# A two-layer graph network: first edge pass over a flat list of tiles, both ends gathered, its network layers a group apart, head sums four tiles at a time

## What is computed

```python
ms, mv = src_s[edge_src] + dst_s[edge_dst], src_v[edge_src] + dst_v[edge_dst]
h = silu(_ln(edge_scalars @ rw1 + rb1, rg1, rbe1))
h = silu(_ln(h @ rw2 + rb2, rg2, rbe2))
w = h @ rw3 + roff                       # 224 weights for each edge
Y1 = SQ3 * edge_vec * rsqrt(sum(edge_vec ** 2))
# products of w with ms, mv, the dot product and the cross product of mv and Y1
ls, lv = _eq_lin(ds, dv, lin_ws, lin_bs, lin_wv)
a = einsum('ehk,hk->eh', _smooth_leaky(alpha), alpha_dot)   # alpha: first 64 columns of ls
a = exp(a - segment_max(a)[edge_dst])    # over all edges with the same destination
ns = segment_sum(vs * a[..., None], edge_dst)     # and nv alike; divided by segment_sum(a)
```

## Time and profile before

| what | us |
|---|---|
| median of 3 runs (range) | 17817.21 (17774.64 to 17817.54) |
| the profiled execution's own time | 17828.81 |
| its span | 17826.9 |
| PE busy | 12392.4 (70%) |
| DVE busy | 10429.4 (59%) |
| ACT busy | 6609.0 (37%) |
| POOL busy | 4214.9 (24%) |
| mean granted TensorE clock | 0.779 of full speed |

### The profile page before, as it was taken

How to read it: one execution, slowest core, us unless ns; L and a number is a source line. 1 busy time by engine, 2 the same in 40 slices (tenths; PEclk the granted TensorE clock), 3 DMA queues, 4 the chain that set the end, 5 groups by cost and what they waited for, 6 DMA issues and landing times. The chain is left out here.

```text
span 17826.9 us, 270188 instructions
## 1 busy us (share of the span) xinstructions
PE 12392.4 (70%) x57506; PEld 9227.4 (52%) x57507; DVE 10429.4 (59%) x31035; ACT 6609.0 (37%) x17353; POOL 4214.9 (24%) x4337
## 2 busy tenths in 40 slices
PE   2488878888878888888862555444457777777776
PEld 1355555555555555555542444433336666666666
DVE  3366666666666666666666555533346666666663
ACT  0244444444444444444430000000025555555552
POOL 0021222122122222122211222200014444444440
PEclk7688888888888888888875666655559988888888
DMA  1121121111122112121222333300014444444443
GB/s 25 33 43 42 41 43 42 41 42 42 41 42 43 42 41 43 41 43 42 43 55 68 76 76 76 68 14 15 16 48 129 129 129 125 128 127 130 125 127 104
DMA packets 1816374, 1150.59 MB, mean 65 GB/s; under 512 B 1159827, under 2 KB 1540793, under 8 KB 1815742
## 3 DMA queue, kind: packets, MB, share of 16 engines
q1 hardware_dynamic: 1641278, 818.30, 17.2%
q0 software_dynamic: 174720, 329.09, 7.8%
HBM read 678.77 MB, written 467.83 MB: 64 GB/s over the span
## 5 line engine op out<-in xcount | busy, mean ns | idle before, releaser
L616 POOL DMA_INDIRECT att_src<-src_table,att_idx x1768 | 1769.4, 1001 | 6823.2 <-DMA att_idx<-in_src_dst 5501.5
L1660 POOL DMA_INDIRECT conv_src<-conv_table,conv_pair x1872 | 1840.6, 983 | 2309.8 <-DVE conv_prod L1820 1759.9
L1748 ACT ACTIVATE conv_scaled<-conv_onehot,conv_pair 128x128 f32<-128x128 f32 x5592 | 1659.1, 387 | 1251.2 <-DVE conv_onehot L1786 761.8
L666 PE MATMUL att_banks<-dst_feat,att_onehotT 128*128 x3528 | 973.0, 372 | 1313.1 <-issue 703.6
L1284 PE MATMUL attend_banks<-attend_wm,attend_onehot 128*128 128x168 f32 x3520 | 1009.3, 476 | 1099.5 <-DVE attend_onehot L1306 1099.5
L1284 PEld LDWEIGHTS attend_banks<-attend_wm,attend_onehot 128*128 128x128 f32 x3520 | 929.7, 320 | 1178.8 <-issue 1063.5
L666 PEld LDWEIGHTS att_banks<-dst_feat,att_onehotT 128*128 128x128 f32 x3528 | 584.0, 210 | 1752.7 <-issue 1752.7
L683 PE MATMUL att_banks<-att_w_last,att_hid 64*128 64x224 f32 x3528 | 1450.0, 499 | 13.0
L1690 PE MATMUL conv_banks<-conv_w_last,conv_hid 64*128 64x224 f32 x1858 | 656.8, 436 | 904.7 <-DVE conv_prod L1820 684.0
L697 PE MATMUL att_banks<-att_ident,att_ch 128*128 128x128 f32 (+1 forms) x5280 | 1240.8, 415 | 2.3 <-ACT att_chT L811 1.4
L1830 DVE SCALAR_TENSOR_TENSOR conv_acc<-conv_acc,conv_keep,conv_banks 128x320 f32<-128x320 f32 x1856 | 898.9, 509 | 541.8 <-PE conv_banks L1712 260.3
(11 more groups left out here) (353 smaller groups left out, 28846.2 us busy)
## 6 DMA issues: line engine op xcount, KB each, us to landing
agg<-conv_acc SPq DMA_DIRECT2D x928, 288.0 KB
messages<-att_msg SPq DMA_DIRECT2D x440, 320.0 KB
attend_msg<-messages SPq DMA_DIRECT2D x220, 640.0 KB, 4.0
conv_pair<-in_conv_rec SPq DMA_DIRECT2D x944, 70.0 KB
att_es<-in_esT SPq DMA_DIRECT2D x1776, 32.0 KB
conv_src<-conv_table,conv_pair POOLq DMA_INDIRECT x1872
att_idx<-in_src_dst SPq DMA_DIRECT2D x1768, 1.0 KB, 1.7
att_geo<-in_edge_vec SPq DMA_DIRECT2D x1768, 1.5 KB
```

Of the source, the lines that this page charges most:

```text
L616: g.indirect_dma_start(out=src[h][:, u, :], out_offset=None, in_=x_table[:, :], in_offset=bass.IndirectOffsetOnAxis(ap=idx[h][:, u, 0:1], ...
L666: last = t.matmul(banks[:, BM, n * FEAT:n * FEAT + FEAT], onehotT[:, u * P:u * P + P], dst_feat[:, bass.ds(b, 1), :].rearrange("p a f -> p ...
L1660: g.indirect_dma_start(out=src[q][:, u, 0, :], out_offset=None, in_=x_table[:, :], in_offset=bass.IndirectOffsetOnAxis(ap=ends[q][:, u // ...
L1748: last = s.activation(scaled[h][:, u, d, :], onehot[h][:, u, :], ACT.Copy, scale=geo[q][:, u // 2, u % 2, PLANE_AT[d]:PLANE_AT[d] + 1])
```

## The change

The first edge pass becomes its own function, `phase_attention`. It walks over a flat list of 1664 tiles (208 iterations of 8), each once, with no step table. The host packs node numbers and edge vectors of 8 tiles in one record and the edge scalars in one block, so that SP starts two loads an iteration, four iterations ahead. `phase_nodes_in` stores the destination rows as a second table in memory, and POOL gathers source and destination rows, 16 indirect DMAs an iteration, into four slots. The one-hots, their transposes and the matmul with `dst_feat` are gone from this loop. `nets` runs layer 1 for one group of 8 tiles and layer 2 for the group before it, so that one `roots` and one `normalise` serve both layers, 1024 columns wide. The hidden features go through the Silu function of another activation table: ACT loads one table ahead of `roots` and the other behind it, in every iteration. `edge_weights` takes rows 0 to 63 and rows 64 to 127 in turn, into two banks. The summing loop works with quads of 4 tiles that share a block: 520 steps of a quad (`QUAD_ITERS` = 130 iterations of 4 quads), PE adds the 4 products of a quad in PSUM, and DVE adds once for each quad. A quad whose edges end in several blocks is taken once for each, as tiles were. The core of the diff:

```diff
-ITERS = -(-(TILES + BLOCKS - 1) // ITER)
-STEPS = ITERS * ITER
-STEP_COLS = -(-(STEPS + 2 * ITER) // P)
-TABLE = STEP_COLS * P
+TURN = 4
+ATT_ITERS = TURN * (-(-TILES // (TURN * ITER)))
+ATT_TILES = ATT_ITERS * ITER
+QUAD = UNIT
+QUADS = ATT_TILES // QUAD
+QUAD_GROUP = 4
+QUAD_ITERS = 2 * (-(-(QUADS + BLOCKS - 1) // (2 * QUAD_GROUP)))
+QUAD_COLS = -(-QUAD_ITERS * QUAD_GROUP // P)
+QUAD_TABLE = QUAD_COLS * P
 NB = 7
 NODE_ITERS = BLOCKS // NB
...
+                    hold(sp, sp_passed, (dst_kept, i + 1))
+                    sp.dma_start(dr[i], out2[:, :, :]).then_inc(stored, 16)
...
-                        v.tensor_tensor(dst_feat[:, bass.ds(i * NB + b, 1), 0:S].rearrange("p a f -> p (a f)"),
-                                        p[:, S:2 * S], bias[:, :], ALU.add)
-                        last = v.tensor_copy(dst_feat[:, bass.ds(i * NB + b, 1), S:FEAT].rearrange("p a f -> p (a f)"),
-                                             p[:, 2 * S + VD:2 * FEAT])
+                        v.tensor_tensor(out2[:, b, 0:S], p[:, S:2 * S], bias[:, :], ALU.add)
+                        last = v.tensor_copy(out2[:, b, S:FEAT], p[:, 2 * S + VD:2 * FEAT])
...
+                def load_edges(it, q):
+                    sp.dma_start(rec[q][:, :, :].rearrange("p u c -> p (u c)"),
+                                 record[bass.ds(it, 1), :, :].rearrange("a p c -> (a p) c")).then_inc(rec_landed[q], 16)
+                    sp.dma_start(es[q][:, :], esA[bass.ds(it, 1), :, :].rearrange("a p c -> (a p) c")).then_inc(es_landed[q], 16)
+
...
+                with sp.Fori(0, TURNS) as i:
+                    for q in range(4):
+                        it = 4 * i + q
+                        for h in range(2):
+                            store(2 * it + h, h)
+                        for used in ((madd_done, 2 * it + 2), (yx_done, it + 1), (x_done, 2 * it + 1)):
+                            hold(sp, sp_passed, used)
+                        load_edges(it + 4, q)
...
+                def gather(k, slot, h, q, turn):
+
+                    hold(pool, pool_passed, (rec_landed[q], 16 * (turn + 1)))
+                    if not isinstance(k, int):
+                        hold(pool, pool_passed, (madd_done, k - 3))
                     for u in range(UNIT):
+                        for rows, table, col in ((srcg, src_table, 0), (dstg, dst_table, 1)):
+                            g.indirect_dma_start(out=rows[slot][:, u, :], out_offset=None, in_=table[:, :],
+                                                 in_offset=bass.IndirectOffsetOnAxis(
+                                                     ap=rec[q][:, UNIT * h + u, col:col + 1], axis=0))\
+                                .then_inc(ends_landed[slot], 16)
...
+                def nets(g, q, turn):
+
+                    pe.wait_ge(es_landed[q], 16 * (turn + 1))
+                    at_least(pe, log_done, g)
+                    t.matmul(banks[:, BX, :], net[0][:, :], es[q][:, :], start=True, stop=True).then_inc(x_done, 1)
+                    at_least(pe, h_done, 2 * g)
+                    t.matmul(banks[:, BX + 1, :], net[1][:, :], hid[0][:, :], start=True, stop=True).then_inc(x_done, 1)
+
+                def means(g):
+
+                    pe.wait_ge(xout_done, 2 * g + 1)
+                    t.matmul(banks[:, BX, :], mean[:, :], sq[:, 0, :], start=True, stop=True)
+                    pe.wait_ge(xout_done, 2 * g + 2)
+                    t.matmul(banks[:, BX + 1, :], mean[:, :], sq[:, 1, :], start=True, stop=True).then_inc(v_done, 1)
+
+                def edge_weights(k, h, it):
+
+                    pe.wait_ge(h_done, 2 * it + 3)
+                    at_least(pe, wev_done, 2 * k)
+                    for c in range(2):
+                        cols = slice((2 * h + c) * P, (2 * h + c) * P + P)
+                        for r in range(2):
+                            rows = slice(r * S, r * S + S)
+                            t.matmul(banks[:, BW + r, c * WN:c * WN + WN], hid[1][rows, cols], w_last[rows, :],
+                                     start=c == 0, stop=False, skip_group_check=True)
+                    for r in range(2):
+                        for c in range(2):
+                            last = t.matmul(banks[:, BW + r, c * WN:c * WN + WN], ones3[:, :], bias3[:, 0, :],
+                                            start=False, stop=True, skip_group_check=True)
                         last.then_inc(w_done, 1)
 
...
+                    at_least(pe, post_done, k)
...
+                with pe.Fori(0, TURNS) as i:
+                    for q in range(4):
+                        it = 4 * i + q
+                        linear(2 * it)
+                        turn_channels(2 * it + 1, 1)
+                        edge_weights(2 * it + 2, 0, it + 1)
+                        linear(2 * it + 1)
+                        edge_weights(2 * it + 3, 1, it + 1)
+                        nets(it + 3, (q + 3) % 4, i + (q + 3) // 4)
+                        turn_channels(2 * it + 2, 0)
+                        means(it + 3)
...
+                def squares(g):
+                    at_least(act, v_done, g)
+                    at_least(act, xn_done, g)
+                    for n in range(2):
+                        act.wait_ge(x_done, 2 * g + n + 1)
+                        s.activation(sq[:, n, :], banks[:, BX + n, :], ACT.Square, bias=net_cols[:, n, 0:1])
+                        s.activation(xb[:, n, :], banks[:, BX + n, :], ACT.Identity, bias=net_cols[:, n, 0:1])\
+                            .then_inc(xout_done, 1)
+
+                def roots(g):
+                    s.preload_act_table_set(TABLES)
+                    act.wait_ge(v_done, g + 1)
+                    s.activation(rs[:, :, :], banks[:, BX:BX + 2, :], ACT.Ln, bias=net_cols[:, 0, 3:4]).then_inc(log_done, 1)
+                    act.wait_ge(log_done, g + 1)
+                    s.activation(rs[:, :, :], rs[:, :, :], ACT.Exp, scale=-0.5).then_inc(rs_done, 1)
+                    act.wait_ge(glen_done, g + 1)
+                    s.activation(glog[:, :], glen[:, :], ACT.Ln).then_inc(glog_done, 1)
+                    act.wait_ge(glog_done, g + 1)
+                    s.activation(glen[:, :], glog[:, :], ACT.Exp, scale=-0.5).then_inc(gr_done, 1)
+                    s.preload_act_table_set(SILU_TABLES)
+
+                def silus(g):
+                    act.wait_ge(xn_done, g + 1)
+                    at_least(act, w_done, 4 * (g - 1) if not isinstance(g, int) else 0)
+                    for n in (1, 0):
+                        if n == 0:
+                            act.wait_ge(x_done, 2 * g + 2)
+                        s.activation(hid[n][:, :], xn[:, n, :], ACT.Silu, scale=net_cols[:, n, 1:2],
+                                     bias=net_cols[:, n, 2:3]).then_inc(h_done, 1)
+
...
+                        s.activation(ea[h][:, us, :], bank[:, :, OUT_S:OUT_S + S], ACT.Silu)
...
+                with act.Fori(0, TURNS) as i:
+                    for q in range(4):
+                        it = 4 * i + q
+                        roots(it + 2)
+                        silus(it + 2)
+                        scalars_out(2 * it, 0, it)
+                        channels_out(2 * it + 1)
+                        weights_out(2 * it + 2)
+                        scalars_out(2 * it + 1, 1, it)
+                        weights_out(2 * it + 3)
+                        squares(it + 3)
+                        channels_out(2 * it + 2)
...
+                def normalise(g):
+
+                    dve.wait_ge(rs_done, g + 1)
+                    at_least(dve, h_done, 2 * g)
+                    v.tensor_tensor(xn[:, :, :], xb[:, :, :], rs[:, :, :], ALU.mult).then_inc(xn_done, 1)
+
+                def endpoints(k, slot, turn, q, h):
+
+                    dve.wait_ge(ends_landed[slot], 16 * 2 * UNIT * (turn + 1))
+                    at_least(dve, prod_done, k)
+                    v.tensor_tensor(m[:, :, :], srcg[slot][:, :, :], dstg[slot][:, :, :], ALU.add).then_inc(madd_done, 1)
...
+                        lengths(it + 2, (q + 2) % 4, i + (q + 2) // 4)
+                        endpoints(k + 2, slots[0], turns[0], coming, 0)
+                        normalise(it + 2)
+                        products(k + 2)
+                        directions(it + 2, (q + 2) % 4)
+                        finish(k, 0, it, q)
+                        weigh(k + 2, 0)
+                        endpoints(k + 3, slots[1], turns[1], coming, 1)
+                        products(k + 3)
+                        weigh(k + 3, 1)
+                        finish(k + 1, 1, it, q)
...
+                    _, ts = nc.values_load_multi_w_load_instructions(
+                        tiles_sb[0:1, bass.ds(G * j, G)], (mybir.EngineType.SP,), min_val=0, max_val=QUADS - 1)
+                    for n in range(G):
+                        us, at = slice(n * QUAD, n * QUAD + QUAD), bass.ds(ts[n] * QUAD, QUAD)
```

(43 more changed lines are left out.)

738 lines of the change are left out of this document (220 added, 518 removed).

## The result

The changed kernel took **14,118.58 us** (median of 4 runs, 14,089.75 to 14,172.79) against 17,815.86 of the kernel before (4 runs). The ratio is 0.7933, with a 95% interval of 0.7906 to 0.7959. I had predicted 13,280 in a range of 12,700 to 14,300. The time is 838 us over the forecast, and that is not the whole story: in later calls the same kernel took 12,303 us.

A forecast was written before the change was run, and what follows sets the result against it. In the attention loop no engine was full and waits between engines filled the rest; DVE paced the summing loop. Terms 45 + 698 + 4992 + 220 + 1050 + 6276 = 13,281, with 2 more 13,283; predicted 13,280 us, range 12,700 to 14,300.

The forecast's parts named there:

- My own forecast: Whole kernel: attention loop periods of 22.5 to 25.8 us, giving 12,950 to 13,700 us, with a chance of 0.62.
- the attention loop: the period: Attention loop: a chain closing through ACT, DVE and PE gives 24.0 us an iteration, 4992 us for 208.
- tighter than the chain: Rival, chance 0.07: clock stays at 2.4 GHz, attention period 21.5 us, summing loop 6.5 us; whole 12,570 us.
- The path that I summed: Attention loop: from `means` through roots, Silus, `scalars_out`, `finish`, `linear` and PE's work back to `means`; 21.5 us before clock and handoffs.
- Transposes: PE in the attention loop: twelve transposes take 2.62 us at full clock, 5.2 us an iteration.
- my bottom of 21: Attention loop: the period can't be under 21 us, with PE at 20.5 and POOL at 20.2.
- Table loads: ACT in the attention loop: two loads of 1.28 us an iteration, the one ahead of `roots` hidden, the other on the chain.
- The rival of dearer loads: Rival, chance 0.17: activations wait twice as long and both table loads count; attention period 26.6 us, whole 13,820 us.
- Coupling as loose as now: Rival, chance 0.10: attention period keeps its ratio to PE work, 1.42, giving 29.2 us; whole 14,360 us.
- Clock stays low: Rival, chance 0.02: half of 2.4 GHz throughout, PE work 41 us, summing loop 9.8 us; whole 17,050 us.
- Summing loop: Summing loop: 130 iterations of 8.0 us, chain of loads 7.1 us; 1050 us in all, 965 less.
- Slower than before: Rival, chance 0.02: gathers of repeated destination rows bound the attention loop; at 3.0 us each, period 48 us, whole 18,270 us.

The follow-up runs named there:

- the kernel that GpSimd doesn't bound: Changed kernel without its eight gathers of destination rows per group of eight tiles (source rows only): 12,231 us, attention loop period 21.5 us.
- the pauses: Changed kernel with a GpSimd memset of 128x512, and a wait for it, after every fourth gather: 13,294 us, beside 12,303 for the changed kernel.
- the second call: Changed kernel 12,303 us, beside versions with records loaded earlier (12,233), destination gathers at source indices (12,296) and a memset after every fourth gather (13,294).
- the fourth: Call with the changed kernel once more, 14,157 us (ratio 0.7956), beside the changed kernel with records loaded an iteration earlier, 14,228 us (ratio 0.8003).
- early records: Changed kernel with SyncE loading records an iteration earlier, before the two stores, and the destination index copied to its own tile: 12,282, 12,233 and 14,228 us.
- My first three kernels: Changed kernel without destination gathers (12,231 us), with destination gathers at source indices (12,344), and with records loaded an iteration earlier (12,282).

## Why the prediction was right, and where it was not

**Right.** The gain, its place and its size by stage: the summing loop within 4 us, the untouched part within 21, softmax within 7, and 3.5 ms of gain expected in the attention loop, of which 2.6 came.

That the range held the time is luck. Its upper part, up to 14,300, stands for dearer table loads and for loose coupling, and neither is what happened. My own forecast, 12,950 to 13,700, held neither 14,119 nor the 12,303 of other calls. Of the signs that I had named, an attention loop of 5.0 ms with PE busy 85% at a clock near 0.9, the result shows 5.9 ms, 69% and 0.85, and the clean kernel 4.6 ms, 82% and 0.95.

**The step that failed** is "the attention loop: the period", 24.0 us. It measured 28.2: 208 times 4.2 is 874 us, of a miss of 838. My list of what would prove me wrong had the sign of it, "if POOL were idle waiting for records". The engine was idle for that, but it wasn't the reason. The term I lacked is late signals, and the trace of the kernel before had them: its 16 remote waits of ScalarE in the attention loop come to 114 us, and those of ScalarE and VectorE behind the summing loop to 428.

```profile
ACT att_ea L821 <- remote: 111.4, 14, 9.2
ACT att_onehotT L793 <- remote: 3.0, 2, 1.5
```

I hadn't looked at them, since they didn't matter in the stage that I was pricing.

**The path that was wrong too.** Without late signals the period is 21.8, 2.2 below my 24.0; the changed kernel then takes 12,303, below my range and near "tighter than the chain" (12,570, 0.07). The path that I summed goes through VectorE's `finish` to `linear`, and it isn't the one that closes: PE waits for `finish` 1.5 us in the whole loop, and for ScalarE's copies of transposes 3.6 us an iteration, where I had 0.6. ScalarE has its roots, Silus and `scalars_out` to do ahead of that copy, so PE's next transposes start 7.9 us after the end of `means` (3009.37, below):

```profile
3017.27 0.64 PE L632 MATMUL att_banks<-att_ident,att_ch 128*96 128x128 f32 x4 [3.10 <-ACT att_chT L721]
```

The sizes were off as well:

- The clock. I took 0.88, that of the convolution loop; it was 0.95, for 1.7 us I should have allowed 0.6.
- Transposes. I read 2.62 us for twelve as their time at full clock. The granted clock of that stretch was 0.50 (the row below). At full clock eight take 1.04 (at 4012.46 above), starts 0.11 apart, so 24 are 2.6 us for my 5.2.
- Edge weights. The four matmuls of a half (eight records) start 0.96 us ahead of the biases (4009.37 and 4010.33 above), and the four biases take 0.40 until L597, where I had worked with 0.58 a pair: 1.36 a half for my 1.76, 0.8 us less an iteration in PE's work.
- PE in all. With these, and 0.87 for each 512-column matmul (4010.73 to 4011.60) where I had 0.97, its work at full clock is about 16.7 us (7.9 + 2.7 + 3.5 + 2.6) for my 20.5.
- GpSimd. I priced a gather at 1.26 (16 are 20.2) by one row; the mean is 1.07 + 0.31, 22.0. This made it the bound, and my bottom of 21 was 1 us too low.

```profile
5002.00:5004.00 2.00, 2.00 (x10) 1.73 (x10) 1.25 (x4) 0.94 (x3) 0.01 (x1) 0.50 0.58 73
```

With the clock, the transposes, the edge weights, the wide matmuls and the load below put right, my path comes to about 19.8 us, an estimate (24.0 - 1.1 - 1.3 - 0.4 - 0.4 - 1.0), under the 21.5 of the kernel that GpSimd doesn't bound. That 24.0 lay between the two measured periods is chance.

**Table loads.** I had the first one hidden and the second on the chain at 1.28. The first was as I said, and the second is nearly hidden too, as a clean iteration shows, ScalarE and then PE's last matmul of `means`:

```profile
3008.30 1.28 ACT L689 ACT_TABLE_LOAD   x1
3009.60 1.11 ACT L691 ACTIVATE att_rs<-att_banks,att_net_cols 128x1024 f32<-128x1024 f32 x1
...
3012.16 1.28 ACT L698 ACT_TABLE_LOAD   x1
3014.55 1.52 ACT L706 ACTIVATE att_hid<-att_xn,att_net_cols 128x512 f32<-128x512 f32 x2 [1.11 <-DVE att_xn L812]
```

```profile
3008.35 1.02 PE L606 MATMUL att_banks<-att_sq,att_mean 128*128 128x512 f32 x2
```

The logarithm (L691) needs `means`, which ends at 3009.37; the load ends at 3009.58, and L691 starts 0.02 behind it. So the load delays it by 0.2 us. Over the clean loop `means` ends 1.07 us after the load starts, on average, and the load adds 0.22 us. Behind the second load ScalarE waits 1.11 more here for VectorE's `xn`; over the loop `xn` comes 1.42 us after that load starts, and the load adds 0.25 us. The rival of dearer loads (26.6 us) is refuted at both. By the rule of the Trainium skill (ScalarE: Activation LUTs, What ACT_TABLE_LOAD costs) each switch would have cost 1.38 more; these rows show no such time.

**The other rivals.** *Coupling as loose as now* (29.2 us) came nearest to the measured period, for a reason that isn't there: with the same orders and the same single banks the clean loop takes 21.8. *Clock stays low* is refuted by 0.85 and 0.95.

**Summing loop.** Right in sum, for another reason than the one given: I had the chain of loads set the pace at 7.1 to 8; GpSimd is busy 885.5 of the 1054 us, 6.8 of each 8.1, where I had 5.3, and so is the engine nearest to the bound. Its two wide products take 5.7 us together (2.87 each), where I had 5.1, and the copy 1.2, where I had 0.2.

**Slower than before** through repeated rows: refuted. With destination rows or with scattered ones, the clean loop took the same 21.8 us, and a gather 1.04 to 1.08.

**What stays open.** Shown: the changed kernel takes 12,303 or 14,157 us, and all of the difference lies in stages with gathers. By stage, gathers per us when clean, and the length with late signals over the clean one: summing 0, 1.00; attention of the kernel before 0.21 (1776 in 8531), 1.01; convolution 0.51, 1.13 to 1.16; attention of the changed kernel 0.72 (3360 in 4637), 1.29. Traffic alone isn't it: the summing loop moves the most, 171 GB/s, without a late signal. Within the first trace, late signals also go with the gathers: spread over their own length, ScalarE's remote waits take 0.23 us per us in the first 12.5 us of a run of gathers (759 us in 3338), 0.62 beyond it (672 in 1092), and 0.17 between runs (254 in 1530). So theory A (late signals come from gathers issued back to back) fits wherever late signals exist. It isn't shown: a correlation doesn't tell which of the two prolongs the other, and the pauses ran only in the clean condition, where 3328 gathers stood back to back without one late signal. Gathers in a row aren't enough; something else comes with them. The record numbers the chips of the calls: 9, 15, 9 and 15, and none for the result. So number 15 had the clean condition in the second call and the late signals in the fourth. If one number is one chip, the chip alone isn't the cause. Within a call the condition didn't change: all 11 runs of the changed kernel and of its early records in the fourth took 14,150 to 14,312. What sets it no run of mine could tell.

## What to carry to other kernels

Put the unchanged kernel into every call of experiments. My first three kernels all seemed to cure the fault, by 13%, and the unchanged one, in calls without late signals, was as fast. Read the granted clock of a stretch before taking a pitch from it as one at full clock: mine was at half. Whether a table load costs anything is told by when the input of the activation behind it is ready, and not by the engine's order alone. When an engine is idle "for a DMA", remove that wait alone before believing it: here the same microseconds came back under another engine's name. And search the trace of before for waits without a near releaser, also in stages that aren't to be changed; a change that doubles the gathers can turn 0.5 us an iteration of them into 8.

## What the runs showed of the hardware

- Late signals: PE's completions reach ScalarE, and in the convolution loop VectorE, microseconds late (13 us at 4026.91), and SyncE's 29-ns moves take up to 712 ns, while ScalarE's and VectorE's own operations keep their durations (L713 542 ns for 541; VectorE busy 3655 us in the loop for 3646), and signals of ScalarE stay within 0.02 us. In the first trace only in the two stages with gathers issued by GpSimd, and not in every call.
- A row gather of 128 rows costs GpSimd 1.04 to 1.08 us and 0.31 until the next, whether rows repeat or not. Halving their number freed it, but the loop gained 0.3 us.
- A 0.54-us memset on GpSimd with a wait for its own semaphore costs 1.2 us.
- A table load is 1.283 us, and the activation behind it starts 0.02 later when its input is ready. The two of an iteration cost 0.22 and 0.25 us, since their activations would have waited for PE and VectorE anyway.
- Twelve fp32 transposes of 128x128 start over 2.62 us at a granted clock of 0.50 to 0.77, and eight take 1.04 us at 1.00.
- Leaving out an explicit load of a table doesn't leave out the load: one came ahead of each change of function, and the kernel lost 1,190 us (13,424 for 12,231).
